# Thirteen batched field pairs instead of ten in a DLRM tower's pairwise-interaction kernel

## The reference

```python
e = jnp.stack([tbl_f[ids[:, f]] for f in range(40)], axis=1)     # 512 x 40 x 64
viW = jnp.einsum('bpd,pde->bpe', e[:, i_idx, :], W)
z = jnp.einsum('bpe,bpe->bp', viW, e[:, j_idx, :])
h = jnp.concatenate([z, dense_ctx], axis=1)
h = jnp.maximum(h @ W_top1 + b_top1, 0.0)
h = jnp.maximum(h @ W_top2 + b_top2, 0.0)
y = h @ W_top3
```

## Time and profile before

| | |
|---|---|
| median of 3 runs | 350.28 us (350.03 to 350.73) |
| the profiled execution | 350.38 us |
| its span, first to last instruction | 348.4 us |
| mean granted clock of TensorE | 0.976 |
| TensorE busy | 320.4 us (92%) |
| VectorE busy | 250.3 us (72%) |
| ScalarE busy | 174.0 us (50%) |
| GpSimd busy | 228.4 us (66%) |

### The profile page before, as it was taken

The page is one execution under the profiler, slowest core; times in us unless marked ns, Lnnn a source line. Parts: engine busy times, 40 slices in busy tenths (PEclk is TensorE's granted clock), DMA queues, the critical chain, the costliest instruction groups (busy, mean ns, idle before and its releaser), DMA issues.

```text
span 348.4 us, 5290 instructions
## 1 busy us (share of the span) xinstructions
PE 320.4 (92%) x1528; PEld 112.4 (32%) x1528; DVE 250.3 (72%) x252; ACT 174.0 (50%) x1312; POOL 228.4 (66%) x192
## 2 busy tenths in 40 slices
PE   0699898529999999999999999999999999999997
PEld 0133432113333333333333333333333333344432
DVE  2385696506887989799899899999998999900000
ACT  1001210000198572876947958795934999190032
POOL 6777777777777734898778884799773994700000
PEclk9999999958999999999999999999999999999969
DMA  6843453323333324933323242322221000000000
GB/s 166 250 149 94 118 131 90 79 49 87 103 95 96 88 77 131 304 83 80 101 67 87 72 109 62 84 68 64 69 66 49 0 3 0 3 0 0 0 0 0
DMA packets 17862, 27.63 MB, mean 79 GB/s; under 512 B 4901, under 2 KB 5029, under 8 KB 17834
## 3 DMA queue, kind: packets, MB, share of 16 engines
q1 hardware_dynamic: 9770, 17.86, 17.8%
q0 software_dynamic: 4608, 4.73, 6.8%
q10 hardware_dynamic: 3456, 4.72, 4.5%
HBM read 22.57 MB, written 0.00 MB: 65 GB/s over the span
## 4 chain that ended last, share of the span: by engine, by line
PE 73%; POOL 16%; issue 6%; DVE 3%; DMA 1%; ACT 0%; DVEq 0%
PE ps_t L539 36%; PE ps_z L561 15%; POOL rows L320 11%; PE ps_t L522 10%; PE ps_t L586 6%; POOL wide_rows L320 5%; PE ps_t L621 3%; DVE prod L447 3%; PE ps_e L501 2%; PE ps_e L586 2%; DMA rows<-in_tbl,ids_sb 1%; DMA ids_sb<-in_ids_t 1%; PE ps_t L627 1%; DVE batched L461 0%; ACT z L393 0%
## 5 line engine op out<-in xcount | busy, mean ns | idle before, releaser
L447 DVE TENSOR_TENSOR prod<-ps_t,E 128x1024 f32<-128x1024 f32 x160 | 184.7, 1217 | 35.6 <-PE ps_t L539 32.0
L372 ACT ACTIVATE batched<-batched 128x64 f32<-128x64 f32 x640 | 152.9, 241 | 23.6 <-DVE prod L447 21.1
L539 PE MATMUL ps_t<-E,w_sb 64*128 64x512 f32 x640 | 156.1, 617 | 1.0 <-DVE prod L447 0.2
L320 POOL DMA_INDIRECT rows<-in_tbl,ids_sb x128 | 121.7, 951 | 38.1 <-issue 37.6
L372 ACT ACTIVATION_READ_ACCUMULATOR batched<-batched 128x1 f32 x640 | 120.0, 188 | 0.0
L327 POOL TENSOR_TENSOR prod<-prod 128x1024 f32<-128x1024 f32 x38 | 89.0, 2371 | 30.0 <-DVE prod L447 29.9
L539 PEld LDWEIGHTS ps_t<-E,w_sb 64*128 64x128 f32 x640 | 55.9, 187 | 90.7 <-issue 60.9
L349 ACT ACTIVATE E<-ps_e 128x512 f32<-128x512 f32 x18 | 10.7, 597 | 102.4 <-PE ps_e L501 79.6
L561 PE MATMUL ps_z<-prod,quads 128*32 128x512 f32 x408 | 58.4, 600 | 0.0
L461 DVE TENSOR_TENSOR batched<-ps_t,wide_rows 128x1024 f32<-128x1024 f32 x40 | 46.2, 1218 | 5.7 <-PE ps_t L522 5.7
L522 PE MATMUL ps_t<-w_sb,E 64*128 64x512 f32 x160 | 37.3, 604 | 0.2 <-DVE batched L461 0.2
(11 more groups left out here) (41 smaller groups left out, 61.2 us busy)
## 6 DMA issues: line engine op xcount, KB each, us to landing
w_sb<-in_w_units SPq DMA_DIRECT2D x50, 256.0 KB, 2.8
E<-E ACTq DMA_DIRECT2D x72, 64.0 KB, 2.6
rows<-in_tbl,ids_sb POOLq DMA_INDIRECT x128
w_sb<-in_w SPq DMA_DIRECT2D x7, 256.0 KB
prod<-in_ids_by_field SPq DMA_DIRECT2D x2, 512.0 KB, 9.1
prod<-in_tbl SPq DMA_DIRECT2D x3, 312.5 KB
w_sb<-in_w SPq DMA_DIRECT2D x1, 512.0 KB
wide_rows<-in_tbl,ids_sb POOLq DMA_INDIRECT x16, 4.8
```

The lines of the kernel that those rows point to most:

```text
L320: pool.indirect_dma_start(rows_of(u, b)[:, f * DIM:(f + 1) * DIM], None, tables[2 * k + f], bass.IndirectOffsetOnAxis(ap=ids_sb[:, col:col ...
L372: last = act.activation(products, products, ACT.Copy, accum_out=zt[:, b, at:at + 1])
L447: dve.tensor_tensor(prod[:, n % P_RING, s, :, :], ps_t[:, step % STEPS, :, :], multiplier, ALU.mult).then_inc(product_ready, 1)
L539: last = pe.matmul(ps_t[:, step % STEPS, j, :], w_sb[at:at + DIM, m % W_RING, col:col + P], E[at:at + DIM, slot_of(pairs_of(n)[s][j]), :], ...
```

## The change

`BATCHED` gets thirteen field pairs, 14 to 0 without 13 and 11, and a list `BATCHED_AT` says behind how many units each stands at the earliest (unit 4 for the first). So 74 groups (37 couples) remain, still 50 units; the last chunk of z that comes from groups holds 10 groups; zt has 208 columns, its second part 80 instead of 32, and the last chunk of h1 uses 96 rows instead of 48. Field pairs up to u = 11 stand one group ahead of their first use (before: up to u = 7), all later ones two groups ahead (before: four). ScalarE has 52 sums instead of 40 and puts one behind every group while any is due. GpSimd adds the halves of 20 couples instead of 19, at other places. The weight ring is 6 instead of 8 deep and `GATHER_LEAD` 14 instead of 12. The two conditions for an incomplete last chunk follow from the 74 groups.

```diff
--- before.py
+++ after.py
@@ -29,12 +29,12 @@
 CODE_RING = 7
 G_RING = 4
 E_RING = 6
-W_RING = 8
+W_RING = 6
 P_RING = 8
 B_RING = 6
 STEPS = 3
 LAG = 7
-GATHER_LEAD = 12
+GATHER_LEAD = 14
 PARAMS_AT = 12
 
 
@@ -43,8 +43,8 @@
 
 
 
-BATCHED = (12, 10, 8, 7, 6, 5, 4, 3, 2, 1)
-BATCHED_FROM, BATCHED_EVERY = 7, (13, 3)
+BATCHED = (14, 12, 10, 9, 8, 7, 6, 5, 4, 3, 2, 1, 0)
+BATCHED_AT = (4, 6, 10, 13, 17, 20, 24, 27, 31, 34, 38, 41, 45)
 
 
 def pair(i, j):
@@ -68,14 +68,14 @@
 NC = NG // 2
 NB = len(BATCHED)
 NU = NC + NB
-CHUNKS = NG // PER_CHUNK
+CHUNKS = -(-NG // PER_CHUNK)
 B_PAIRS = 2 * WIDE * NB
 B_REST = B_PAIRS - P
 ALL_CHUNKS = CHUNKS + 2
 DENSE_AT = B_REST
 
 
-ADDED_COUPLES = (12, 13, 15, 18, 20, 21, 23, 25, 26, 27, 28, 30, 32, 33, 34, 35, 36, 37, 38)
+ADDED_COUPLES = (10, 14, 15, 16, 18, 19, 20, 21, 23, 24, 25, 26, 27, 28, 30, 31, 32, 33, 34, 35)
 ADDED = [n for n in range(NG) if n // 2 in ADDED_COUPLES]
 
 
@@ -94,7 +94,7 @@
 
 
 def ahead(u):
-    return 1 if u < 8 else 4
+    return 1 if u < 12 else 2
 
 
 SPLIT_FIRST = (0, 2, 3, 1)
@@ -121,8 +121,7 @@
         if n in WIDE_AFTER:
             yield "rows", WIDE_AFTER.index(n)
         units += n % 2
-        if n % 2 and j < NB and arrival(BATCHED[j]) < u and units >= (
-                BATCHED_FROM + BATCHED_EVERY[0] * j // BATCHED_EVERY[1]):
+        if n % 2 and j < NB and arrival(BATCHED[j]) < u and units >= BATCHED_AT[j]:
             yield "batched", j
             j += 1
             units += 1
@@ -382,7 +381,7 @@
                     copy_rows(at)
                 elif kind == "batched":
                     left += [(at, b) for b in range(BT)]
-                elif kind == "group" and left and at % 7 in (0, 2, 3, 5):
+                elif kind == "group" and left:
                     sum_batched(*left.pop(0))
             assert len(left) <= (B_REST // (2 * WIDE)) * BT
             act.wait_ge(zt_turned, 1)
@@ -464,7 +463,7 @@
                                       ALU.mult).then_inc(product_ready, 1)
 
             def copy_z(c):
-                dve.wait_ge(two_reduced, PER_CHUNK // 2 * (c + 1))
+                dve.wait_ge(two_reduced, min(PER_CHUNK // 2 * (c + 1), NC))
                 dve.tensor_copy(z[:, c, :], ps_z[:]).then_inc(z_copied, 1)
 
             for kind, at in order():
@@ -560,7 +559,8 @@
                             to = 32 * (2 * (g % 2) + j)
                             last = pe.matmul(ps_z[to:to + 32, :], ones, prod[:, g % P_RING, s, j, :],
                                              start=(q == 0 and s == 0),
-                                             stop=(q == PER_CHUNK // 2 - 1 and (s == 1 or g in ADDED)))
+                                             stop=((q == PER_CHUNK // 2 - 1 or n == NG - 2)
+                                                   and (s == 1 or g in ADDED)))
                 last.then_inc(two_reduced, 1)
 
             pe.wait_ge(ident_ready, 1)
```

## The result

| | before | after |
|---|---|---|
| median, us | 350.50 (350.03 to 351.04, 4 runs) | 355.56 (354.51 to 357.27, 4 runs) |
| ratio after / before | | 1.0149, 95% interval 1.0096 to 1.0201 |
| profiled execution (span), us | 350.38 (348.4) | 354.51 (352.3) |
| ScalarE busy, us | 174.0 | 219.1 |
| TensorE busy, us | 320.4 | 316.6 |

The kernel became slower by 1.5%. TensorE has less to do than before and still ends later.

A forecast was written before the change was run, and what follows sets the result against it. TensorE was the bound before; after the change ScalarE's in-order list of sums and copies would be. 350.38 + 6.5 (VectorE's products end later) - 3.4 (tail) = 353.5, less 0.1 for the median: 353.4, range 350.8 to 358.0.

The forecast's parts named there:

- Start of the list: ScalarE's first sum begins at 67.5, including 1.95 us charged for low clock after TensorE's 7.4 us gap.
- Length of the list: On ScalarE, 48 sums (183.8), eleven copies with DMA issues (34.1) and one without (0.6) take 218.5 us without a break.
- four close calls: Places where ScalarE nearly idles: copies of u=8, 10 and 15 and sum 24, with leads of 0.8 to 2.8 us.
- Waits of TensorE: TensorE waits for ScalarE's copies: about 5 us for u=9, some 2 for 10 and 14, under 2 for 11 and 19.
- Rival (c): ScalarE idles, or TensorE's 3 to 5 us waits lower the clock; each microsecond goes onto the end: 359, chance 0.07.
- From C19 to the last product: From the start of ScalarE's copy of field pair k=0 (286.0) to VectorE's end at 311.5, 6.5 us later than before.
- The tail: After the last products, the clock holds with 96 rows instead of 48 in h1's last chunk: -3.4 us.
- Where the TensorE savings went: On TensorE, 6.4 us of reductions and 7.3 us of units saved are all lost in waits for ScalarE's copies.
- rival (d): ScalarE is not the bound and TensorE sets the time: 341, or 338 with the tail's 3.4; chance 0.09.
- The spacing of ScalarE: ScalarE's sums take 3.83 us each, 0.24 per piece of 64, from the trace; the skill's numbers gave 2.3 per sum.
- One sign: In the new profile, ScalarE stands at 9 in nearly every slice from 67 to 305.

The follow-up runs named there:

- the run with SyncE's queue: The changed kernel with the four DMAs behind each ScalarE copy issued by SyncE's queue instead of ScalarE's, from field pair u=4 on: 339.93 us, ratio 0.971.
- the control run: The kernel before with the four DMAs behind each ScalarE copy issued by SyncE's queue, from field pair u=4 on: 350.34 us, ratio 1.0007.

## Why the prediction was right, step by step

**The mechanism held**: a wait for ScalarE takes the place of TensorE's work. The forecast of 353.4 stood for a profiled execution of 353.5; that came at 354.51. The median came at 355.56, 2.2 us over the forecast; the steps below are those of the profiled execution, the fastest of four.

- **Start of the list.** s0 was put at 67.5 and came at 66.51. The rows of u=6 landed 0.6 us sooner, and the low clock cost 1.5 us instead of 1.95: from 56.39 to 63.98 are 7.59 us, at the prices of the earlier trace rows 6.08.
- **A wrong reason there.** I wrote that the new lead puts C6 ahead of g6. The lead of u=6 is one group in both kernels. It is the batched unit of k=14 that does it: it takes two groups out of that field pair, so the first use of u=6 moves from g9 to g7. The number was not touched by it.
- **Length of the list.** 218.5 was forecast, 219.8 measured. Of the difference, 0.7 are C7's DMA issues (3.16 instead of 2.44) and 0.6 the wait ahead of s24, one of the four close calls named. C19: 286.0 forecast, 286.27 measured. It came so close in part by luck: the start was 1.0 early and the list 1.3 long.
- **Waits of TensorE.** For C9 5 us were forecast and 4.91 came; for C10 and C14 some 2 each, and 0.88 and 2.53 came; for C11 under 2, and 0.56 came; for C19 under 2, and 3.31 came. Rival (c) speaks of 3 to 5 us for C19, which does not go with that forecast; the rival had it right.
- **From C19 to the last product.** 25.5 forecast, 26.2 measured. This is rival (c) in small: the wait of 3.31 let the clock fall (0.55 from 288 to 291), and B12 took 5.2 us instead of 3.63. In the run with SyncE's queue, where the wait was 0.60 and B12 took 3.74, the same stretch is 25.3. I gave this only 0.07 and no part in the sum.
- **The tail.** It was to be 3.4 us shorter, with the clock holding over 96 rows. From VectorE's last product to the end are 42.0 us, 45.4 before; the run with 96 rows on the kernel before shows that the rows alone do it.
- **Where the TensorE savings went.** 13.7 us were counted as saved and lost in waits. With ScalarE freed the kernel came at 339.9, where rival (d) put it with the tail's gain (338) to within 2 us. That fits savings that were real and only covered up.
- **The spacing of ScalarE.** The Trainium skill's numbers ("ScalarE: Activation LUTs", What ACT_TABLE_LOAD costs) had made rival (d) of it. Sums still start 3.83 us apart in the changed kernel; the run with one piece less shows that this spacing is what the kernel pays for. One sign was put wrongly: ScalarE was to stand at 9 in nearly every slice, and the page has 6 to 8 there about as often, since DMA issues do not count there.

**What stays open.** The four runs of the changed kernel lie at 354.51, 354.52, 356.61 and 357.27. The profile is of the first. The mean granted clock of the four is 0.976, 0.976, 0.966 and 0.962 in that order. The profile has three falls of the clock that follow TensorE's waits for copies, and more or longer ones would give such a spread, but no profile of one of the two longer executions shows it.

## What to carry to other kernels

An engine that is half busy on average can become the bound when every item of its list stands ahead of something that another engine waits for: add up its list in program order from the first item that is due to the last that is awaited, DMA issues included, before work is moved onto it. The engine can hold the others up by a buffer that it frees late as well as by a copy: with the old lead it was a tile of the ring. Shortening the lead of a copy is safe only while the engine that makes it has no backlog. Work that needs no arithmetic, as issuing a DMA, is the first to move off such an engine.

## What the runs showed of the hardware

- Four DMA issues on ScalarE cost it 2.44 us behind most copies (3.16 behind C7), near the price of 10 summed pieces (0.24 each). From SyncE's queue they cost the kernel nothing that its time shows: the control run is at 1.0007.
- TensorE's clock fell to 0.50, the lower of its two levels (1.2 of 2.4 GHz), behind eight instructions of 48 rows and held at 1.00 behind the same eight with 96 rows, with the same wait of 0.68 us ahead of them. It fell in the tail of all three profiles with 48 rows and of none of the seven with 96. Filling up the rows with zeros gained 2.4 us of 350.
- Waits of TensorE cost more than their own length here: behind waits of 4.91 and 3.31 us the granted clock was 0.50 and 0.55, and a batched unit took 4.94 and 5.20 us to the start of the next, while behind waits of 0.96 and 0.60 it took 3.74.
